# Loading weights one stage ahead in a two-layer decoder: early projection and gated attention

## What is computed

```python
x = ln(x + l0_attn(x)); x = ln(x + l0_xattn(x, ctx)); x = ln(x + l0_ffn(x))
xn = ln(x) * ln_w + ln_b
v  = silu(xn @ v_w.T + v_b)
mx = silu(conv(xn, k) + xn * omega)              # k from ema_delta, ema_alpha, ema_beta, ema_gamma
base = mx @ mx_w.T + mx_b                        # u, z, r, hx are slices of it
h  = silu(hx + (softmax(q @ k.T + bias) @ v * r) @ h_w.T + h_b)
x  = ln(x + (x + u * (h - x)))
k1, v1 = ctx @ Wk.T + bk, ctx @ Wv.T             # of layer 1's cross attention; needs only ctx
x  = ln(x + l1_xattn(x, k1, v1)); x = ln(x + moe(x))
```

## Time and profile before

| | us |
|---|---|
| median of 3 runs (2752.1 to 2754.99) | 2754.79 |
| the profiled execution, its own time | 2750.7 |
| its span | 2749.0 |
| busy PE / DVE / ACT / POOL | 2367.3 / 1401.6 / 1113.6 / 933.3 |
| mean DMA rate | 114 GB/s |

### The profile page before, as it was taken

One profiled execution on the slowest core, in us unless ns is written; L12 is line 12 of the kernel. 1 busy time (PEld: TensorE's weight loads), 2 busy tenths in 40 slices (PEclk: granted clock), 3 DMA queues, 4 the chain that ended last, 5 costly groups with the idle time before them and its releaser, 6 DMA issues. The chain is left out here.

```text
span 2749.0 us, 44609 instructions
## 1 busy us (share of the span) xinstructions
PE 2367.3 (86%) x17103; PEld 1815.4 (66%) x17134; DVE 1401.6 (51%) x2497; ACT 1113.6 (41%) x1898; POOL 933.3 (34%) x897
## 2 busy tenths in 40 slices
PE   9688887799995768978898869999995799999993
PEld 4466666466664546745665658887884688888883
DVE  5599898387775940003544536787776011111113
ACT  2466665356554644434333235555452111111113
POOL 2455554234443770000101024565556122222221
PEclk9799999899998889999999989999997899999997
DMA  2133324300101668552121033433431765666634
GB/s 73 53 103 117 116 98 146 108 16 24 47 16 58 211 173 205 160 182 93 31 62 46 16 133 99 106 97 97 117 88 43 291 188 180 177 184 190 191 85 134
DMA packets 227409, 313.11 MB, mean 114 GB/s; under 512 B 76672, under 2 KB 209792, under 8 KB 214016
## 3 DMA queue, kind: packets, MB, share of 16 engines
q1 hardware_dynamic: 201888, 253.82, 29.7%
q0 software_dynamic: 16352, 18.69, 3.8%
q10 hardware_dynamic: 8960, 37.75, 3.6%
HBM read 187.58 MB, written 122.63 MB: 113 GB/s over the span
## 5 line engine op out<-in xcount | busy, mean ns | idle before, releaser
L2548 ACT ACTIVATE me_h<-me_ps_h 128x512 f32<-128x512 f32 x156 | 93.1, 597 | 461.6 <-PE me_ps_h L2528 461.6
L2585 DVE TENSOR_SCALAR me_yo<-me_ps_y,me_mt 128x256 f32<-128x256 f32 x78 | 37.8, 484 | 473.6 <-PE me_ps_y L2537 454.8
L2528 PE MATMUL me_ps_h<-me_xt,me_w 128*128 128x256 f32 x1248 | 277.0, 380 | 0.0
L2537 PE MATMUL me_ps_y<-me_w,me_h 128*128 128x256 f32 x1248 | 275.6, 379 | 0.0
L2473 POOL DMA_INDIRECT xo<-me_yo,me_row x78 | 121.8, 1562 | 452.8 <-DVE me_yo L2585 306.9
L2537 PEld LDWEIGHTS me_ps_y<-me_w,me_h 128*128 128x128 f32 x1248 | 237.1, 190 | 32.2
L2528 PEld LDWEIGHTS me_ps_h<-me_xt,me_w 128*128 128x128 f32 x1248 | 235.1, 191 | 30.6
L327 POOL TENSOR_TENSOR l0ah_cm<-l0ah_c,l0ah_after 128x1024 f32<-128x1024 f32 x64 | 151.7, 2370 | 174.3 <-DVE l0ah_c L392 174.3
L666 POOL TENSOR_TENSOR l0x_en<-l0x_e,l0x_ri 128x1024 f32<-128x1024 f32 x64 | 120.0, 1896 | 210.7 <-DVE l0x_ri L888 210.7
L2036 POOL TENSOR_TENSOR l1x_e<-l1x_e,l1x_ri 128x1024 f32<-128x1024 f32 x64 | 121.8, 1902 | 195.6 <-DVE l1x_ri L2302 194.2
L987 PE MATMUL kv_ps<-kv_w_v,kv_ct 128*128 128x512 f32 x256 | 120.2, 609 | 24.7 <-PEq L82 15.3
(11 more groups left out here) (381 smaller groups left out, 5303.0 us busy)
## 6 DMA issues: line engine op xcount, KB each, us to landing
me_w<-in_w SPq DMA_DIRECT2D x39, 2048.0 KB, 8.6
xs<-dec_zero SPq DMA_DIRECT2D x31, 1024.0 KB, 4.6
k<-kv_kt ACTq DMA_DIRECT2D x16, 1024.0 KB, 7.0
v<-kv_va ACTq DMA_DIRECT2D x16, 1024.0 KB, 6.1
l1x_kt<-k SPq DMA_DIRECT2D x16, 1024.0 KB, 7.3
l1x_va<-v SPq DMA_DIRECT2D x16, 1024.0 KB, 5.8
me_xg<-xs SPq DMA_DIRECT2D x39, 256.0 KB, 8.6
l0ap_x<-in_x SPq DMA_DIRECT2D x32, 128.0 KB, 2.0
```

The costliest lines, as they stand in the source:

```text
L2528: last = pe.matmul(ps_h[i % HB][:, f % 2, :], w[:, j % WB, FFN * c + f * P:FFN * c + f * P + P], xt[:, j % 2, c, :], start=c == 0, stop=c ...
L2537: last = pe.matmul(ps_y[q][:, 0:D], h[:, j % 2, f, q * P:(q + 1) * P], w[:, j % WB, W2 + D * f:W2 + D * f + D], start=f == 0, stop=f == FC ...
L2548: act.activation(h[:, j % 2, 2 * i:2 * i + 2, :], ps_h[i % HB][:, :, :], ACT.Gelu).then_inc(gelued, 1)
```

## The change

Three things. (1) The projection's tiles and semaphores are opened before l0_xattn, whose SP now issues the projection's weights and its first two context loads behind its own last loads; FFN_FIRST becomes 10, so ten pieces are made ahead of the FFN's first group, and ACT keeps them in the order 0 and 1, squares of group 0, weights, 2 to 4, squares of group 1, 5 to 9. (2) The gated attention's weights, small tensors and input tiles move into a class GatedAttentionInput (mw_...), opened before l0_ffn. mega_conv's SP loads the 13 weights and group 0 of xn between the toep stores and the wait for them, and group 0 of mx after the stores of mx have landed. (3) To make room, tiles are shared: l0_xattn scales e in place, so that its exponential waits for the transposes of two tiles before in place of the scaling; the gated attention's v, r, hr, df and wg lie in the projection's kt, va, weights, cx and ct. The projection's and the new class's semaphores are cleared after mega_attn, in two blocks of their own.

```diff
 l0_xattn, gpsimd, scalar and sync
-                    slot_free(pool, e_transposed, n, 2, 4)
                     item_done(pool, inverted, n)
-                        pool.tensor_tensor(en[:, n % 2, u, :, :], e[:, n % 2, u, :, :], spread(ri[:, n % 2, u, :], P),
+                        pool.tensor_tensor(e[:, n % 2, u, :, :], e[:, n % 2, u, :, :], spread(ri[:, n % 2, u, :], P),
...
-                    slot_free(act, e_scaled, n, 2, 2)
+                    slot_free(act, e_transposed, n, 2, 4)
...
                     if g + 3 < NG:
                         load(g + 3)
+                    if g + 3 == NG:
+                        kv.load_weights(sp)
+                        for early in range(2):
+                            kv.load_ctx(sp, early)
                     if g >= 1:
                         store(g - 1)
...
+class GatedAttentionInput:
+    def load_weights(self, sp):
+        m = self.m
+        loads = [(self.w_z, m["wz"]), (self.w_v, m["wv"]), (self.w_r, m["wr"]), (self.w_uh, m["wuh"]), (self.w_h, m["wh"])]
...
+    def load(self, sp, c, src, g):
+        tiles = src.rearrange("l (t b) d -> t l b d", b=BQ)
+        for t in range(self.G):
+            sp.dma_start(self.xin[:, g % 2, c, t, :], tiles[self.G * g + t, :, :, :]).then_inc(self.xin_loaded[c][g % 2], 16)
...
-FFN_FIRST, FFN_STEP = 1, 5
+FFN_FIRST, FFN_STEP = 10, 5
...
 l0_ffn, sync and scalar
-                kv.load_weights(sp)
...
-                for g in range(2):
-                    kv.load_ctx(act, g)
...
+                kv.keep(act, 0, 2)
                 sum_squares(0)
                 act.wait_ge(w_loaded, 5 * 16)
                 act.activation(w[:, :, :], w_i[:, :, :], ACT.Copy).then_inc(w_ready, 1)
-                kv.keep(act, 0, FFN_FIRST)
+                kv.keep(act, 2, 5)
                 sum_squares(1)
+                kv.keep(act, 5, FFN_FIRST)
...
 mega_conv, sync
                                  kp[:, :, L - 1 - l:2 * L - 1 - l]).then_inc(pad_stored, 16)
+                mw.load_weights(sp)
+                mw.load(sp, 0, xn, 0)
                 sp.wait_ge(pad_stored, 16 * L)
...
                 sp.wait_ge(stored, 16 * G)
+                mw.load(sp, 1, mx_out, 0)
...
 mega_attn
-        v = kit.sb("v", [P, 2, G, HV])
-        r = kit.sb("r", [P, 2, 4, GP])
+        v = kv.kt[:, :, :, :].rearrange("p u (t c) n -> p u t (c n)", t=G)
+        r = kv.va[:, :, :, :].rearrange("p u t (c n) -> p u (t c) n", c=2)
...
-                load(0)
-                sp.dma_start(zp[:, :], m["zp"]).then_inc(w_loaded, 16)
...
 decoder_stages
         mega_attn(nc, x3, xn, mx, kv, mw, x4)
         kv.kit.clear_semaphores()
+        mw.kit.clear_semaphores()
```

More of the change, by code:

```diff
@@ L912, in l0_xattn, with __init__ @@
         kit.clear_semaphores()
+L, BM, Z, HV, NE = B, S, 128, 512, 16
+BQ = P // L
+class GatedAttentionInput:
+    G = 4
+    def __init__(self, nc, stack, m):
+        kit = Kit(nc, stack, "mw")
+        self.m, self.kit = m, kit
+        self.w_v, self.w_r, self.w_uh = (kit.sb(n, [P, 2, HV]) for n in ("w_v", "w_r", "w_uh"))
+        self.w_z = kit.sb("w_z", [P, 2, Z])
+        self.w_h = kit.sb("w_h", [P, 4, D])
+        self.b_v, self.b_uh = kit.sb("b_v", [P, HV]), kit.sb("b_uh", [P, HV])
+        self.b_h = kit.sb("b_h", [P, D])
+        self.b_r = kit.sb("b_r", [P, 4])
+        self.zp = kit.sb("zp", [P, 5])
+        self.rot = kit.sb("rot", [P, 2, L])
+        self.ab = kit.sb("ab", [P, 2, 2])
+        self.same = kit.sb("same", [P, P])
+        self.xin = kit.sb("xin", [P, 2, 2, self.G, D])
+        self.w_loaded = kit.sem("w_loaded")
+        self.xin_loaded = [[kit.sem(f"{c}_loaded{u}") for u in range(2)] for c in ("xn", "mx")]
+    def load_weights(self, sp):
+        m = self.m
+        loads = [(self.w_z, m["wz"]), (self.w_v, m["wv"]), (self.w_r, m["wr"]), (self.w_uh, m["wuh"]), (self.w_h, m["wh"])]
+        for dst, src in loads:
+            sp.dma_start(dst[:, :, :], src.rearrange("(k p) n -> p k n", p=P)).then_inc(self.w_loaded, 16)
+        for dst, src in ((self.b_v, m["bv"]), (self.b_uh, m["buh"]), (self.b_h, m["bh"])):
+            sp.dma_start(dst[:, :], bcast(src)).then_inc(self.w_loaded, 16)
+        sp.dma_start(self.zp[:, :], m["zp"]).then_inc(self.w_loaded, 16)
+        sp.dma_start(self.b_r[:, :], m["br"]).then_inc(self.w_loaded, 16)
+        sp.dma_start(self.rot[:, :, :], m["rot"]).then_inc(self.w_loaded, 16)
+        sp.dma_start(self.ab[:, :, :], m["ab"]).then_inc(self.w_loaded, 16)
+        sp.dma_start(self.same[:, :], m["same"]).then_inc(self.w_loaded, 16)
+    W_LOADS = 16 * 13
+    def load(self, sp, c, src, g):
+        tiles = src.rearrange("l (t b) d -> t l b d", b=BQ)
+        for t in range(self.G):
+            sp.dma_start(self.xin[:, g % 2, c, t, :], tiles[self.G * g + t, :, :, :]).then_inc(self.xin_loaded[c][g % 2], 16)
 class EarlyKeysValues:
@@ L925, in __init__ @@
         self.ident = kit.sb("ident", [P, P])
-        self.w_k, self.w_v = (kit.sb(n, [P, 2, H * self.W]) for n in ("w_k", "w_v"))
+        self.w_kv = kit.sb("w_kv", [P, 2, 2, H * self.W])
+        self.w_k, self.w_v = self.w_kv[:, 0, :, :], self.w_kv[:, 1, :, :]
         self.b_k = kit.sb("b_k", [P, self.C])
@@ L938, in __init__, with take_banks @@
         self.kit = kit
+    def take_banks(self, kit):
+        self.ps = [kit.ps(f"ps_kv{i}", [P, 2 * self.GP]) for i in range(2)]
     def piece(self, n):
@@ L1528, in mega_attn @@
          normed) = (kit.sem(n) for n in names)
-        xin_loaded = [[kit.sem(f"{c}_loaded{u}") for u in range(2)] for c in ("xn", "mx")]
         x_loaded = [kit.sem(f"x_loaded{u}") for u in range(3)]
@@ L1535, in tiles @@
             return a.rearrange("l (t b) d -> t l b d", b=BQ)
-        loads = [(w_z, m["wz"]), (w_v, m["wv"]), (w_r, m["wr"]), (w_uh, m["wuh"]), (w_h, m["wh"])]
-        rows = [(b_v, m["bv"]), (b_uh, m["buh"]), (b_h, m["bh"])]
-        W_LOADS = 16 * (len(loads) + len(rows) + 5)
         with nc.Block() as block:
@@ L1545, in load @@
                     slot_free(sp, xt_ready, g, 2, 4)
-                    for c, src in ((1, mx_in), (0, xn_in)):
-                        for t in range(G):
-                            sp.dma_start(xin[:, g % 2, c, t, :], tiles(src)[G * g + t, :, :, :]).then_inc(xin_loaded[c][g % 2], 16)
+                    mw.load(sp, 1, mx_in, g)
+                    mw.load(sp, 0, xn_in, g)
                 def load_x(g):
@@ L1559, in store @@
                         sp.dma_start(tiles(x_out)[G * g + t, :, :, :], y[:, g % 2, t, :]).then_inc(stored[g % 2], 16)
-                load(0)
-                sp.dma_start(zp[:, :], m["zp"]).then_inc(w_loaded, 16)
-                for dst, src in loads:
-                    sp.dma_start(dst[:, :, :], src.rearrange("(k p) n -> p k n", p=P)).then_inc(w_loaded, 16)
-                for dst, src in rows:
-                    sp.dma_start(dst[:, :], bcast(src)).then_inc(w_loaded, 16)
-                sp.dma_start(b_r[:, :], m["br"]).then_inc(w_loaded, 16)
-                sp.dma_start(rot[:, :, :], m["rot"]).then_inc(w_loaded, 16)
-                sp.dma_start(ab[:, :, :], m["ab"]).then_inc(w_loaded, 16)
-                sp.dma_start(same[:, :], m["same"]).then_inc(w_loaded, 16)
                 for n in range(1, NG + 3):
```

49 lines of the change are left out of this document (20 added, 29 removed).

## The result

The changed kernel took 2733.93 us in the median of five runs against 2752.43 for the kernel before on the same chip: a ratio of 0.993, with a 95% interval of 0.9919 to 0.9942. One of the five, the one that was profiled, was a disturbed execution of 3234.83 us, which the ratio leaves out (the other four took 2731.34 to 2734.89). Measured again the changed kernel took 2729.38 against 2752.69, 0.9914 (0.99 to 0.9927).

The account below looks back on a forecast made before the run. Stretch by stretch: POOL paces the FFN, PE the convolution's tail, weight loads the gated attention's start. Terms -14.7 - 1.0 - 16.2 + 9.0 + 0.6 = -22.3 us gave 2728.4 profiled, 2732 as median; range 2724 to 2738.

Parts of the forecast that it names:

- Part 1, the tail: Convolution's tail, bound by PE: nine projection pieces fewer, a gain of 14.7 us.
- Part 1, the FFN's start: Start of the FFN, where the nine pieces go: first residual at 906.5, 1.2 us earlier; taken as -1 us.
- POOL's pace hands it on to the stage's end: FFN: the 1 us gained at the first residual carries through to the end of the stage.
- Part 2, the attention's start: Start of the gated attention, weights and inputs already in SBUF: 22.3 us become 6.1, gain 16.2, bounds 12 to 18.8.
- Part 3, mc_t: Convolution: the 17 early loads ahead of the four mc_t loads delay them, +9 us, bounds 6.5 and 12.
- The first rival: Convolution: the mc_t loads drain behind the weights on one queue, +12 to +13 us, so 2736; chance 0.18.
- Part 4: The rest, such as in-place scaling, early cross attention loads, shared tiles and semaphore clears: +0.6 us net.
- The FFN was not held up: Rival at the FFN's start: early pieces at half clock delay the first residual 10 to 12 us, 2743; chance 0.06.
- the convolution didn't starve: Rival in the convolution: weights run at the toep stores' 34 GB/s, time about 2826; chance 0.04.
- The stage's start waited for nothing late: Rival at the gated attention's start: it waits for late mx, part 2 gives only 5, 2743; chance 0.07.
- mc_t's wait: Sign in the convolution: PE idle before its first mc_ps near 15 us instead of 6.37; above 22 the forecast is wrong.
- POOL stayed at 0.89: Sign in the FFN's steady part: the forecast is wrong if POOL is no longer near 0.89 busy.

Follow-up runs that it names:

- experiment 3: Changed kernel with FFN_FIRST back at 1 and ACT's former order at the FFN's start; weights stay early: 2748.08 us, 0.9981 of the kernel before.
- experiment 2: Changed kernel with the gated attention's weights and xn inputs issued behind the four mc_t loads instead of ahead: 2719.71 us, 0.9877 of the kernel before.
- experiment 4: Changed kernel with the gated attention's weights and group-0 inputs loaded in its own stage again: 2738.99 us, 0.9948 of the kernel before.
- experiment 10: Changed kernel with only the four xn loads moved behind mc_t, the weights staying ahead: 2731.79 us, 0.9925 of the kernel before.
- experiment 9: Changed kernel with only the 13 weight loads moved behind mc_t, the four xn loads staying ahead: 2724.6 us, 0.9899 of the kernel before.
- experiment 7: Changed kernel with the 13 weight loads issued by POOL at the convolution's start, xn by SP behind mc_t: 2724.62 us, 0.9897 of the kernel before.
- experiment 5: Changed kernel with CONV_AFTER 48 for 40, moving eight pieces from the convolution's tail ahead of mc_t's wait: 2722.52 us, 0.9887 of the kernel before.
- experiment 6: Changed kernel with weights and xn behind mc_t and CONV_AFTER 45 for 40, five more pieces ahead of mc_t's wait: 2717.37 us, 0.9872 of the kernel before.
- experiment 12: Changed kernel with weights and inputs behind mc_t and FFN_STEP 6 for 5, eight more pieces in the FFN: 2714.16 us, 0.9858 of the kernel before.
- experiment 1: The changed kernel unaltered, run again for a profile at the usual clock: 2729.38 us, 0.9914 of the kernel before.
- experiment 11: Changed kernel with the weights issued by SP in the FFN's steady part and xn behind mc_t: 2720.96 us, 0.9888 of the kernel before.

## Why the prediction was right, and where it was not

Forecast 2732, measured 2733.93 and 2729.38. As differences to the kernel before, the forecast is -22.3 us, and the two measurements have -18.5 and -23.3. The sum is also the profile's (-22.1), but in part by luck: the FFN's start (1.3 off) and mc_t (3.6 off) cost more than forecast, and the clock in the gated attention, which is not in the sum, gave 4.0. The stated range of 2724 to 2738 doesn't come out of the bounds either; added up, these give 2727 to 2744.

**Part 1, the tail (-14.7): right.** -14.6 in the profile, and 14.5 when experiment 3 takes it back.

**Part 1, the FFN's start (-1): wrong in size, and its conclusion in kind.** The timelines of PE, ACT and DVE there, which answer to the earlier trace rows:

```profile
882.91 1.11 PE L1025 MATMUL ffn_ps_kv<-kv_ident,kv_cx 128*128 128x128 f32 x4 [9.96 <-ACT ffn_identb L1248]
884.80 7.59 PE L1034 MATMUL ffn_ps_kv<-kv_ct,kv_w_kv 128*128 128x256 f32 x24 [0.78 <-ACT kv_ct L1062]
...
902.39 0.61 PE L1296 MATMUL ffn_ps_t<-ffn_identb,ffn_xq 128*128 128x128 bf16 x8
...
889.32 0.41 ACT L1255 ACTIVATE ffn_sq<-ffn_x 128x256 f32<-128x256 f32 x1
...
891.24 0.17 DVE L1374 TENSOR_SCALAR ffn_wsd<-ffn_ws 128x4 f32<-128x4 f32 x1 [17.16 <-DMA ffn_lnb<-in_mlnb]
...
892.58 0.16 DVE L1322 TENSOR_SCALAR ffn_st<-ffn_sums 128x4 f32<-128x4 f32 x1
...
906.28 1.65 DVE L1355 SCALAR_TENSOR_TENSOR ffn_r<-ffn_ps_y,ffn_st,ffn_xb 128x256 f32<-128x256 f32 x4
```

PE's ten pieces fill 883 to 903, as named, and the residual is at 906.28 (forecast 906.5). It comes 13.70 us behind DVE's mean square (892.58), where it was 13.68, so by that distance it still hung on the DVE chain; the forecast had PE as the later of the two. And the stage began 0.94 earlier, so from its start the residual came at 24.41 in place of 24.95 us, 0.5 earlier and not 1.2, and the stage as a whole was 0.3 longer. "POOL's pace hands it on to the stage's end" did not hold. What stays true is that nine more pieces cost the FFN under 1 us (0.8 against experiment 3).

**Part 2, the attention's start (-16.2): right.** 5.12 us are left where 6.1 were summed, as the transposes ran in one piece; -17.2, inside the bounds of -12 to -18.8.

**Part 3, mc_t (+9): too small.** This is the step that failed: "nearest the issue row, since DMA stands partly free there". With the loads in place the DMA engines were full (1.01 to 1.03), and the 17 loads that were to be issued in 9.9 us took 12.6 (experiment 3) to 14.1 from the end of the toep row to mc_t. The profile has +12.6, though the kernel before had the shortest such stretch of the seven profiles with nothing ahead of mc_t (74.05 to 78.72, median 76.7); against that median the changed kernel's 86.60 is +10, and experiments 2 and 4 give 9 to 10. Counted from the end of the toep row (table at experiment 10) it is 11.2 and 13.1. So the term is 9 to 13. The kind of delay was right: mc_t is issued later (73.50 us into the stage, not 61.90). Once issued, it is no slower than without the loads: 13.10 us to mc_ps, 12.61 and 13.99 in experiments 3 and 10, against 12.15 to 14.61 in the seven. The first rival had it issued at the forecast's time and then held up behind the weights; its price of 12 is within the range, but that picture isn't in the rows. What both left out is that the issue itself is slower while the DMA engines are full: the four xn loads took 5.42 us and alone 2.53 (experiment 9). Most of the cost is the weights': 3 MB put mc_ps off by 8.6 us against experiment 2 (86.31 - 77.74), which is 350 GB/s, or by 9.6 against the median.

The Trainium skill (DMA: Bandwidth & Descriptors, Queues, rings and completion order) has descriptors consumed in ring order on each engine; by that rule the sum had 12. The measured 9 to 13 hold both 9 and 12 and decide nothing by size, and since mc_t took no longer behind the weights once issued, no run here shows the ring order at work.

A queue of its own helped little: in experiment 7 the weights went by POOL's, and mc_ps still came 8.7 us later than that median. The mc_xg loads took 15 us more to issue, of which the rows behind them won back a part.

**Part 4: near.** The in-place scaling costs nothing that can be told (1.0002). The two clears show in POOL's wait ahead of layer 1's cross attention, 6.47 us in place of 5.36: +1.1 against a net +0.6. POOL's timeline, before and then changed:

```profile
1588.98 0.20 POOL L111 MEMSET l1x_ident<- 128x128 f32 x1 [5.36 <-POOLq L82]
```

```profile
1566.11 0.20 POOL L111 MEMSET l1x_ident<- 128x128 f32 x1 [6.47 <-POOLq L82]
```

The +0.8 behind that, in stages with the same instructions, has no cause that a run shows.

**Not in the sum: the attention's clock, -2.3 and -1.7.** In its last group the kernel before has a row of eight products at 5.40 us where the changed kernel's takes 3.70 (last section). That 1.7 and the clears' 1.1 make the -0.6 of the table. Without the clock the profile's gain would be 18.1.

**The rivals.** The FFN was not held up, and the convolution didn't starve: the weights ran at 368 to 379 GB/s, not near the toep stores' 34. The stage's start waited for nothing late: the mx loads were issued at 1194.15, 28.7 us ahead of it, where 10 were forecast. Of the signs named, one missed: mc_t's wait was 17.64 us, not "near 15", still under the 22 that would have made the forecast wrong. POOL stayed at 0.89 in the FFN's steady part.

## What to carry to other kernels

A load that is moved ahead of its use is only free if nothing that an engine waits for stands behind it or beside it: put it behind the awaited load on its queue. Here the same 17 DMAs cost 10 us four instructions earlier and next to nothing behind mc_t. The time to issue such loads, read where the DMA engines have room, is only a floor: here it said 9.9 us, and 12.6 to 14.1 passed; work it out by the bytes and the rate that the trace shows as well. Work put into the resulting idle time can lengthen the wait if it uses the DMA engines too: it seems to have done so in experiment 5, and did not in experiment 6, where the weights were behind mc_t.

Filling work is cheapest in a stage that another engine paces: in experiment 12 eight pieces cost 13 us in a tail where PE is alone, and 0.7 us where DVE and POOL set the step.

## What was not expected of the hardware

**A full queue slows the issue of the next loads.** The four xn loads took 5.42 us to issue behind the weights and 2.53 without them, 6.38 in experiment 5 with more stores beside them; experiment 7's mc_xg loads 42.45 against 27.07. A long row of the queue in the timeline can then be a sign of other traffic, not a price of the DMA.

**The same pause may cost clock or not.** In each of the last six of the gated attention's eight groups PE pauses 2.49 us for a vector operation ahead of a row of ma_ps_v. In the kernel before, PE's timeline (the third and the last group) and the window over the first of the two rows:

```profile
1324.14 5.40 PE L1821 MATMUL ma_ps_v<-ma_w_v,ma_xt 128*128 128x512 f32 x8 [2.49 <-DVE ma_vb L1697]
...
1531.00 5.40 PE L1821 MATMUL ma_ps_v<-ma_w_v,ma_xt 128*128 128x512 f32 x8 [2.48 <-DVE ma_vb L1697]
```

```profile
1324.00:1328.00 4.00, 3.86 (x5) 1.70 (x6) 0.83 (x3) 1.17 (x2) 2.23 (x2) 0.57 0.00 0
```

And in the changed kernel the same groups:

```profile
1303.60 3.70 PE L1852 MATMUL ma_ps_v<-mw_w_v,ma_xt 128*128 128x512 f32 x8 [2.49 <-DVE ma_vb L1728]
...
1508.71 3.70 PE L1852 MATMUL ma_ps_v<-mw_w_v,ma_xt 128*128 128x512 f32 x8 [2.48 <-DVE ma_vb L1728]
```

```profile
1304.00:1308.00 4.00, 4.00 (x16) 2.20 (x15) 1.49 (x3) 1.43 (x3) 1.68 (x1) 1.00 0.00 0
```

Before, the granted clock falls to nearly its lower level (0.57) behind the pause, and the eight products take 5.40 us; in the changed kernel it stays at 2.4 GHz and they take 3.70. Of the six such pauses in the kernel before, two cost this and four don't; in the changed kernel none does. Of the thirteen profiles (with that of the kernel before) four (column e at 108.9) have no such dip in the first three groups, and nine lose 2.0 to 4.3 us: 1.6 or 1.7 by the dip, the rest at the stage's start, where the clock comes back later (between 4 and 8 us into the stage it is 0.96 in experiment 1, 0.70 in experiment 3, 0.50 in experiment 6). The instructions there are the same in all, and kernels that reach the stage within 1 us of each other (experiments 9 and 11: 1213.37 and 1214.05) fall on both sides. No run here settled what decides it. The start of the FFN spreads as well, from 879.83 to 883.62 us over the eleven changed kernels, which have the same instructions up to there. Both are as large as several of the differences that were to be measured, and show that a difference of spans under some 5 us has to be read by stretches before it is put down to an edit.
